# Weighting the values once per four heads, with all work of the attention stage placed by tables

## The reference

```
x = x + attention(layernorm(x), ctx, ctx, mask) @ wo
x = x + experts_and_shared_ffn(layernorm(x))
attention: scores = rope(q) rope(k)^T / sqrt(32), softmax over 512 keys, times v
```

## Time and profile before

| | |
|---|---|
| median of 3 runs | 1559.9 us (1558.6 to 1561.17) |
| the profiled execution | 1558.8 us |
| its span, first to last instruction | 1557.0 us |
| PE busy in the span | 1451.6 us, 93% |
| DVE, ACT, POOL busy | 955.2, 910.6, 532.4 us |
| attention stage, by the tiles' transposes | 68.3 to 854.8 us |

### The profile page before, as it was taken

One profiled execution on the slowest core, in us unless ns is written; L12 is line 12 of the kernel. 1 busy time (PEld: TensorE's weight loads), 2 busy tenths in 40 slices (PEclk: granted clock), 3 DMA queues, 4 the chain that ended last, 5 costly groups with the idle time before them and its releaser, 6 DMA issues. The chain is left out here.

```text
span 1557.0 us, 37250 instructions
## 1 busy us (share of the span) xinstructions
PE 1451.6 (93%) x11434; PEld 1179.1 (76%) x11434; DVE 955.2 (61%) x2635; ACT 910.6 (58%) x2050; POOL 532.4 (34%) x665
## 2 busy tenths in 40 slices
PE   4699999999999989999989489999999999999997
PEld 3487787887887868878767367888888888888885
DVE  4487777867778778687766366666565333333332
ACT  2389888887889878888897232222221344444442
POOL 2133232331432314223222143222224455546553
PEclk9799999999999999999999789999999999999999
DMA  4234345444354443544434513222225877886652
GB/s 153 68 110 127 110 122 160 124 133 125 110 163 124 137 130 113 154 120 131 129 99 145 190 64 82 82 89 81 91 80 168 238 194 178 203 232 118 111 89 35
DMA packets 141482, 198.94 MB, mean 128 GB/s; under 512 B 34903, under 2 KB 72543, under 8 KB 141282
## 3 DMA queue, kind: packets, MB, share of 16 engines
q1 hardware_dynamic: 120738, 157.81, 33.3%
q0 software_dynamic: 17952, 33.64, 11.6%
q10 hardware_dynamic: 2592, 4.98, 0.9%
HBM read 97.10 MB, written 69.35 MB: 107 GB/s over the span
## 5 line engine op out<-in xcount | busy, mean ns | idle before, releaser
L896 DVE CUSTOM_DVE_ANT_0 a_probs<-a_psum,a_bias 128x512 f32<-128x512 f32 x512 | 348.6, 686 | 168.4 <-PE a_psum L711 156.8
L528 ACT ACTIVATE a_probs<-a_probs,a_low 128x512 f32<-128x512 f32 x512 | 369.0, 721 | 105.4 <-DVE a_low L896 101.2
L623 PE MATMUL a_psum<-a_ident,a_probs 128*128 128x128 f32 x2048 | 318.2, 278 | 19.3 <-DVE a_xT_lo L843 6.2
L623 PEld LDWEIGHTS a_psum<-a_ident,a_probs 128*128 128x128 f32 x2048 | 242.7, 141 | 90.7 <-issue 38.3
L711 PE MATMUL a_psum<-a_kT,a_q_stack 128*128 128x512 f32 x512 | 249.5, 488 | 9.1 <-DMA a_q_stack<-a_qT_lo 5.6
L534 ACT ACTIVATE a_probsT<-a_psum 128x512 f32<-128x512 f32 x400 | 234.2, 586 | 12.1 <-issue 6.6
L1246 POOL DMA_INDIRECT out<-b_y,b_pairs_sb x71 | 113.2, 1594 | 147.2 <-DMA out<-b_y,b_pairs_sb 87.2
L730 PE MATMUL a_psum<-a_probsT,a_v 128*32 128x128 f32 x4096 | 139.6, 277 | 7.4 <-ACT a_probsT L534 4.7
L1689 DVE SCALAR_TENSOR_TENSOR b_v_hidden<-b_v_hidden,b_psum 128x256 f32<-128x256 f32 x71 | 29.9, 421 | 165.3 <-ACT b_v_hidden L1348 165.3
L730 PEld LDWEIGHTS a_psum<-a_probsT,a_v 128*32 128x32 f32 x4096 | 105.1, 110 | 30.0 <-issue 17.4
L446 POOL CAST a_w_hi<-a_w_raw 128x256 fp32r<-128x256 f32 x96 | 38.6, 402 | 259.4 <-DMA a_w_raw<-in_L_ffn_Wd 126.3
(11 more groups left out here) (206 smaller groups left out, 3156.6 us busy)
## 6 DMA issues: line engine op xcount, KB each, us to landing
b_w<-w_halves SPq DMA_DIRECT2D x16, 1536.0 KB
a_q_stack<-a_qT_hi SPq DMA_DIRECT2D x256, 64.0 KB, 2.0
a_q_stack<-a_qT_lo SPq DMA_DIRECT2D x256, 64.0 KB, 2.0
w_halves<-a_w_hi SPq DMA_DIRECT2D x96, 128.0 KB, 1.8
w_halves<-a_w_lo SPq DMA_DIRECT2D x96, 128.0 KB, 1.9
a_x_in<-in_x SPq DMA_DIRECT2D x32, 256.0 KB, 2.9
a_ctx_in<-in_ctx SPq DMA_DIRECT2D x32, 256.0 KB, 3.9
a_x_res<-in_x SPq DMA_DIRECT2D x32, 256.0 KB, 3.0
```

Of the source, the lines that this page charges most:

```text
L528: nc.scalar.activation(probs[:, h % 2, t], probs[:, h % 2, t], ACT.Exp, bias=low[:, h % H, t:t + 1], scale=-1.0, accum_out=total[:, h // G ...
L623: last = nc.tensor.transpose(out[:, P * i:P * (i + 1)], src(i), identity[:])
L896: nc.vector.tensor_tensor_reduce(probs[:, h % 2, t], psum[:, t % 2], bias[:, t], 1.0, HUGE, ALU.add, ALU.min, low[:, h % H, t:t + 1]).then ...
```

## The change

It does four things in the attention stage.

- `weighted` takes a number of query tiles; it is called once per group with all four, so the moving operand has 512 columns in four pieces of 128 (`turned`), and a call still has 32 matmuls. It stands at position u = 17, 33, 49 of the batch and at u = 1 of the next, which is 5 tiles after the group's last head began.
- `probsT` has two spare slots in place of four, and its slots are numbered by head and then by tile, so that the four pieces lie at even distances (or in two pairs, for the first head of an odd group).
- Tables (`PE_AT`, `ACT_AT`, `DVE_AT`) say beside which tile each of the other operations stands on each engine; the loops run over the 64 tiles. The order scores, transposes and evacuation keep among themselves is the same, six tiles ahead. `qT` 2 now stands at u = 21 on PE, and `q_low` 2 at u = 22 on DVE.
- DVE evacuates 20 tiles of a batch in place of 14. POOL's `finish_q`, `finish_k` and `inverse_root` move by a head or so. SP's list is unchanged.

In the end part the last group's call comes after the transpose of the inverse sums and before `spread`, where three calls stood around `spread`.

```diff
-DOUBLED = (0, 1, 1, 2)
-DVE_EVACUATES = ((3,), (1,), (), (3,), (3,), (), (), (3,), (1,), (3,), (), (1,), (1, 3), (3,), (1, 3), (3,))
+AHEAD = 6
+DOUBLED = (1, 1, 0, 0)
+OUT_STEPS = ((0, 4, 5),)
+DVE_EVACUATES = ((1,), (2,), (1,), (), (2, 3), (), (), (3,), (0, 1, 3), (1, 3), (), (1, 3), (0, 3), (0,), (1, 3), (1, 3))
+PE_AT = {
+    1: (('out', -1),), 2: (('inverse', -1),), 4: (('spread', -1),), 6: (('xT', 0),), 7: (('ctxT', 0),), 10: (('q', 0), ('q', 1)), 11: (('q', 2),),
+    12: (('q', 3),), 13: (('xT', 1),), 14: (('kv', 0),), 15: (('q', 4),), 17: (('out', 0),), 18: (('inverse', 0), ('q', 5)),
+    19: (('ctxT', 1), ('q', 6)), 20: (('spread', 0),), 21: (('xT', 2), ('qT', 2), ('q', 7)), 23: (('q', 8),), 24: (('q', 9),),
+    25: (('kT', 0), ('q', 10)), 26: (('q', 11),), 27: (('xT', 3),), 28: (('kv', 1),), 29: (('q', 12), ('q', 13)), 31: (('ctxT', 2), ('q', 14)),
...
+}
+ACT_AT = {
+    4: (('inverse', -1),), 8: (('spread', -1),), 12: (('xT', 0),), 15: (('ctxT', 0),), 26: (('xT', 1),), 30: (('att_hi', -1),), 36: (('inverse', 0),),
+    38: (('ctxT', 1),), 40: (('spread', 0),), 42: (('xT', 2),), 43: (('qT', 2),), 54: (('xT', 3),), 62: (('att_hi', 0),), 63: (('ctxT', 2),),
...
+}
+DVE_AT = {
+    1: (('stats', 0),), 2: (('moments', 0),), 5: (('xn', 0), ('att', -1)), 7: (('x_low', 0),), 8: (('stats', 1),), 9: (('moments', 1),),
+    10: (('xn', 1),), 11: (('inverse', 0),), 12: (('q', 0),), 13: (('x_low', 1),), 15: (('stats', 2), ('kv', 0), ('moments', 2)), 17: (('xn', 2),),
+    20: (('stats', 3),), 21: (('att', 0), ('q', 1), ('x_low', 2)), 22: (('q_low', 2),), 23: (('moments', 3),), 24: (('xn', 3),), 25: (('kT', 0),),
...
+}
...
+            if DOUBLED == (1, 1, 0, 0):
+                return t if i == 0 and t < 2 and h // GH % 2 else 2 + TT * i + t
...
+        def turned(h, t, tiles, c):
+
+            at = [ring(h, i) for i in range(t, t + tiles)]
+            step = at[1] - at[0] if tiles > 1 else 1
+            if all(b - a == step for a, b in zip(at, at[1:])):
+                return probsT[:, at[0]:at[-1] + 1:step, P * c:P * (c + 1)]
+            apart = at[2] - at[0]
+            pairs = probsT[:, at[0]:at[0] + 2 * apart].rearrange("p (a b) l -> p a b l", a=2)
+            return pairs[:, :, 0:2, P * c:P * (c + 1)]
...
-                            last = nc.tensor.matmul(psum[DK * j:DK * (j + 1), OUT, P * t:P * (t + 1)], v[:, batch, c, DK * (h // REP):DK * (h // REP + 1)],
-                                                    probsT[:, ring(h, t), P * c:P * (c + 1)], start=(c == 0), stop=(c == TT - 1))
-                    if t == TT - 1:
+                            last = nc.tensor.matmul(psum[DK * j:DK * (j + 1), OUT, P * t:P * (t + tiles)], v[:, batch, c, DK * (h // REP):DK * (h // REP + 1)],
+                                                    turned(h, t, tiles, c), start=(c == 0), stop=(c == TT - 1))
+                    if t + tiles == TT:
                         last.then_inc(s["out_filled"], 1)
...
+                    for u in range(H * TT):
+                        evacuate(b, u // TT, u % TT)
+                        beside(part, b, par, 2 * u)
+                        if u + AHEAD < H * TT or part != "last":
+                            exp(b, (u + AHEAD) // TT, u % TT ^ 2)
+                        beside(part, b, par, 2 * u + 1)
...
+                    for u in range(H * TT):
+                        turn_probs(part, b, u // TT, u % TT)
+                        if u + AHEAD < H * TT or part != "last":
+                            scores(b, par, (u + AHEAD) // TT, u % TT ^ 2)
+                        beside(part, b, par, u)
...
+                    for u in range(H * TT):
+                        evacuate(b, u // TT, u % TT)
+                        if u + AHEAD < H * TT or part != "last":
+                            lowest(b, (u + AHEAD) // TT, u % TT ^ 2)
+                        beside(part, b, par, u)
```

More of the change, by code:

```diff
@@ L142, in attention_phase @@
[L142 to L146, removed]
         STORE = {10: 0, 12: 1, 14: 2}
         RESIDUAL = {3: 0, 4: 1, 11: 2, 13: 3}
-        K_HEADS = {4: 0, 7: 1, 10: 2, 12: 3}
+        X_HEADS = {0: 0, 2: 1, 3: 2, 5: 3}
@@ L150, in attention_phase @@
+        Q_HEADS = {3: 0, 5: 1, 6: 2, 8: 3}
+        K_HEADS = {3: 0, 7: 1, 9: 2, 12: 3}
+        LOW_HEAD = 3
         PIECE_HEAD = 3
[L152 to L177, removed]
+        def there(part, kind, i):
+            if kind in ("inverse", "spread", "out", "att", "att_hi"):
+                return part in ("middle", "last") or part == "first" and i >= 0 or part == "end" and i < 0 and kind != "out"
+            if kind in ("qT", "q_low"):
+                return part in ("first", "middle") or part == "last" and i < HG
+            if kind in ("wo", "add"):
+                return part in ("middle", "last")
+            if kind == "probs":
+                return part in ("first", "middle", "last")
+            return part in ("first", "middle")
@@ L179, in group_done, with stages @@
+        def stages(part, table, at):
+            return [(kind, i) for kind, i in table.get(at, ()) if there(part, kind, i)]
         def group_done(part, h):
@@ L205, in upto @@
             return b * per + (ahead * per + i + 1)
+        RINGED = ("xT", "ctxT", "kv", "kT", "qT", "inverse", "spread")
         line = []
[L208 to L212, removed]
+        for u in range(H * TT):
+            line.append(("probs", u))
+            line += [(kind, i) for kind, i in PE_AT.get(u, ()) if kind in RINGED]
         assert len(line) % len(RING) == 0
@@ L758, in beside @@
                             spread_inverse(part, b, i)
-                    if pos == 1 and weighted_at(part, h):
-                        weighted(b, par, *weighted_at(part, h))
-                    products()
+                        if kind == "out":
+                            for t, tiles, after in OUT_STEPS:
+                                if (GH * i + GH - 1) * TT + after == u:
+                                    weighted(b, par, i, t, tiles)
+                        if kind == "q":
+                            project_q(part, b, i // DC, i % DC)
+                        if kind == "wo":
+                            project_out(part, b, par, i // DC, i % DC)
                 def body(part, b, par):
@@ L784, in body @@
                         turn_inverse(part, b, -1)
[L785 to L786 removed]
+                        for t, tiles, after in OUT_STEPS:
+                            if TT * (GH * HG - 1) + after >= H * TT:
+                                weighted(b, par, -1, t, tiles)
                         spread_inverse(part, b, -1)
[L788 removed]
                         for t in range(TT):
```

182 lines of the change are left out of this document (55 added, 127 removed), and 4 rows, old and new, of the table PE_AT.

## The result

The changed kernel takes 1611.8 us (median of 4 runs, 1609.2 to 1613.7) against 1560.5 us beside it (1558.6 to 1563.9): ratio 1.0325, 95% interval 1.0304 to 1.0346. Forecast were 1538 us. The change is slower by 51 us.

What follows compares the result with a forecast made beforehand. PE was taken to bound the middle batches, busy 98.25 of 102.5 us. From 1558.8 us, less 27.6 for the calls, plus 1.5 at the end and 4.2 of stalls, came 1536.9, as median 1538; range 1518 to 1556.

Steps and rivals of the forecast that it cites:

- the part on the q stack: `qT` 2 moved to u = 21 makes PE wait 2.2 us per batch at u = 26; work behind SP's wait costs nothing.
- the first head's 7.4 us: Time from q's transposes to a usable head: 3.4 us to the low part, 3.9 for four issues and landing.
- The long call: One call of `weighted` per group takes 3.57 us, 3.71 with going in and out; the group saves 0.89 us.
- The Trainium skill's figures: 131 ns per 512-column matmul against 81 per 128-column one: a long call of 1.63 us, some 90 us saved; not adopted.
- The pieces of the moving operand: Four pieces of 128 columns in the long call: taken as no cost, at most 0.9 us per group, +28 us.
- The wait at u = 26: PE waits for `q_stack` once per batch at head 8's scores: 2.2 us taken, 1 to 3 to be seen.
- The stalls: PE's idle time per middle batch goes from 4.3 to 4.9 us (1.6 + 2.2 + 1.1), +4.2 us over 7 batches.
- the end part: After the last group's call, `spread` and its copy are uncovered: +1.5 us.
- The forecast's stall on ACT before the call at u = 17: Between the calls at u = 1 and 17 ACT needs 3.6 us more than PE; PE stalls 1.6 us.
- the saving: Fewer surroundings of calls of `weighted`: 0.89 us per group, 27.6 us over the 31 groups inside the batches.
- Rival C: Slower: the long call starves ACT and DVE, PE idles 8.6 us per batch, 4.3 more than now; 1563 us, chance 0.10.
- The mark that I had set: The prediction is wrong if, among other signs, PE's idle time per batch is above 7 us.

Runs made afterwards that it cites:

- Experiment 4: The changed kernel with the turn of q for group 2 back at u = 15 in place of 21, copy and low half with it: 1561.6 us.
- 6: The kernel before with one edit, the turn of q for group 2 at tile 22 in place of 15: 1625.7 us, ratio 1.0415.
- 13: The changed kernel with two buffers for a raw weight piece in place of one: 1582.5 us, ratio 1.0142.
- 14: The changed kernel with two buffers for a raw weight piece and the turn of q for group 2 back at u = 15: 1552.6 us, ratio 0.9942.
- experiment 1: The kernel before with the long call alone, at tile 17 of the group with two spare slots, all else in its old place: 1586.3 us, ratio 1.0169.
- q_pool: The changed kernel with weight pieces' transfers issued from GpSimd in place of SyncE, and the turn of q for group 2 back at tile 15: 1621.8 us.

## Why the prediction was wrong

**The step that failed** is the last sentence of the part on the q stack: "Behind SP's wait for `q_low` 2 are a weight piece, a residual and ctx 3: all have ten tiles or more left, so nothing." I looked at when each of them is read, and not at the queue. What stands behind SP's wait are also three more heads of the stack, which must be out before `qT_hi` is free for group 3, and the piece's reader is POOL, whose list holds `finish_k` and the inverse roots behind it. Experiment 4 prices the late turn at 50 us in the changed kernel, 6 at 65 in the old one. Experiments 13 and 14 split the 50 roughly, as differences of times: some 20 us run through the pieces (the second buffer is worth 29 us with the late turn and 9 without), and 30 are left with two buffers (1582.5 to 1552.6).

The measured time is 74 us over the forecast. The late turn has 50 of them; the other 24 are a gain that didn't arrive, since experiment 4 stands at 1561.6 where 1538 was forecast.

The sum could have been made from rows that I had. From turn to low part 3.4; sixteen transfers of 0.6, 9.8; the last landing, 2.0. That is 15.2 us before anything stands between them, and three pieces, a residual and ctx do. The trace has 22.2 us for the whole. Eleven tiles are 17.5 us (303.95 to 321.49). I worked out the first head's 7.4 us and stopped there.

**What was right.** The long call: 3.57 us, 0.41 at both sides, 3.57 a batch off PE's list at full clock. The Trainium skill's figures ("TensorE: Matmul & The Clock Gate", section "Back-to-back issue gap"), by which the call would have been 1.63 us, don't hold for these fp32 strips: 32 matmuls of 512 columns take 3.57 us where 32 of 128 take 1.01. The pieces of the moving operand cost nothing that shows. The wait at u = 26: 0.92 us here and 1.2 in the mean of the 8 new ones, where 2.2 was taken and 1 to 3 were to be seen.

**What was off besides.** The stalls: 4.9 us forecast a batch, 11.7 idle here. The placement of `kv` 3 and `kT` 3 has no term in the sum, and PE's wait for `k_stack` is the longest. The price of the lower clock behind a wait has none either. It shows in the end part, too: from the inverse sums to the first product there were 6.64 us and are 8.44, 1.8 more where 1.5 was forecast, but the products behind that gap begin at half clock (0.50 from 909.0 to 914.4 us) and take 2.5 us more. The forecast's stall on ACT before the call at u = 17 isn't among the waits of `L728`. Of the saving I took it that it arrives wherever PE has no gap; experiment 1 shows that in the old places it doesn't. Even with the queue's slack restored (14) the kernel gained 8 us, 5.7 against the kernel before with the same buffers, where the calls alone were to save 27.6. The rest went into waits of the new places (PE stands 8.0 us in the batch at 258 us, 4.25 in that of the earlier trace rows): at the turn of the loop (4.15 us), and by 0.81, 0.61 and 0.97 us at u = 6, 9 and 23. Rival C had the sign but not the cause. The mark that I had set, more than 7 us idle per batch, was passed.

**Open.** Which of the new places makes up for the 26 us that the long call loses in the old ones wasn't taken apart. Nor why PE's branch at the loop's turn comes later in some of these kernels than in others (waits put down to issue of 3.3 to 7.3 us).

## What to carry to other kernels

When a step moves, follow every queue it releases to the end of what it has to issue, count the issues of all its transfers, and compare with the distance to the step that reuses its buffer, not only to its first reader. A transfer queue that waits in order holds everything behind it, so work that nobody is waiting for (weights for a later stage) can stop the critical engine through a third one. Give such background work a second buffer before a table is tightened: it cost 1 KB a partition and was worth 29 us under a late turn.

## What the runs showed of the hardware that was not expected

- A transfer of q of 64 KB costs SP's queue 0.6 us to issue (1.18 and 1.22 us for two) and the transfer lands 2.0 us after its issue (median): sixteen per group are 9.8 us of SP, and four groups 39 of a batch of 102.5.
- Issued from POOL, a piece's transfers took 0.54 to 0.56 us each of POOL's own time (medians in `q_pool`), against 0.34 to 0.44 mostly on SP.
- After PE had stood for 4.52 us, the next 6.8 us ran at a granted clock of 0.50, the four transposes at 0.72 us from start to start in place of 0.36. PE took 6.27 us there (358.99 to 365.26) for what takes some 3.4 at full clock, an estimate from the rows there (transposes 0.36, scores 0.32 to 0.41, a product 0.70): the wait of 4.52 us cost some 2.8 more behind it.
